# ScalarE instead of VectorE copies the transposed rows out of PSUM in the projections, and the query pieces go ahead of the keys' cast

## What is computed

```python
qh = split_heads(layernorm(x) @ Wq + bq)      # 16 x 512 x 256
kh = split_heads(ctx @ Wk + bk)               # 16 x 1601 x 256
vh = split_heads(ctx @ Wv + bv)
scores = einsum('bhqd,bhkd->bhqk', qh, kh) * 16 ** -0.5
out = einsum('bhqk,bhkd->bhqd', sparsemax(scores), vh)
x = x + tanh(g_xattn[0]) * (merge_heads(out) @ Wo + bo)
x = x + tanh(g_ffn[0]) * moe(layernorm(x))    # 8 experts, the best 2 of each row
```

## Time and profile before

| | us |
|---|---|
| median of 3 runs | 6868.18 |
| lowest and highest | 6863.97, 6875.29 |
| the profiled execution | 6908.67 |
| its span, first to last instruction | 6906.8 |

### The profile page before, as it was taken

One profiled execution on the slowest core, in us unless ns is written; L12 is line 12 of the kernel. 1 busy time (PEld: TensorE's weight loads), 2 busy tenths in 40 slices (PEclk: granted clock), 3 DMA queues, 4 the chain that ended last, 5 costly groups with the idle time before them and its releaser, 6 DMA issues. The chain is left out here.

```text
span 6906.8 us, 164803 instructions
## 1 busy us (share of the span) xinstructions
PE 5085.9 (74%) x19554; PEld 1673.0 (24%) x19555; DVE 6013.8 (87%) x50066; ACT 5556.3 (80%) x12484; POOL 2471.6 (36%) x10299
## 2 busy tenths in 40 slices
PE   8895777776777677676777777777777777767695
PEld 5551111111111111111111111111111111136574
DVE  4558999999999999999999999999999999957445
ACT  3336998998999999898999999999999999942221
POOL 2222333333333333333333333333333333324432
PEclk9995676676667766666766676666666676677798
DMA  5762111111111111111111111111111111145235
GB/s 194 238 201 56 30 34 29 31 35 28 31 31 32 31 31 31 30 30 29 28 31 32 31 32 31 33 29 31 31 35 32 32 32 33 28 152 207 89 100 204
DMA packets 691615, 415.98 MB, mean 60 GB/s; under 512 B 503712, under 2 KB 597536, under 8 KB 690208
## 3 DMA queue, kind: packets, MB, share of 16 engines
q1 hardware_dynamic: 677408, 370.58, 21.4%
q0 software_dynamic: 13056, 35.74, 1.4%
HBM read 249.13 MB, written 156.88 MB: 59 GB/s over the span
## 5 line engine op out<-in xcount | busy, mean ns | idle before, releaser
L887 DVE MAX8 a_cand<-a_scores 128x8 f32<-128x42 f32 (+1 forms) x38912 | 4395.9, 199 | 176.8 <-issue 140.9
L633 ACT ACTIVATE a_junk_act<-a_cand,a_ntau 128x304 f32<-128x304 f32 (+1 forms) x3840 | 1933.4, 522 | 145.2 <-POOL a_ntau L964 49.7
L603 PE MATMUL a_ring<-a_q,a_k 99*128 99x512 bf16 (+1 forms) x3328 | 1472.0, 556 | 764.1 <-ACT a_scores L669 499.3
L548 PE MATMUL a_out<-a_attn,a_v 128*32 128x512 f32 (+1 forms) x6656 | 1418.0, 793 | 518.8 <-ACT a_attn L673 518.8
L669 ACT COPY a_scores<-a_ring 128x1024 f32<-128x1024 f32 (+1 forms) x2048 | 1611.3, 830 | 154.0 <-PE a_ring L599 83.5
L673 ACT ACTIVATE a_attn<-a_ring 128x1024 f32<-128x1024 f32 (+1 forms) x1792 | 1654.1, 975 | 52.1 <-PE a_ring L603 50.9
L599 PE MATMUL a_ring<-a_k,a_q 96*128 96x512 bf16 (+1 forms) x4096 | 1336.5, 454 | 75.9 <-DVE a_ident L700 33.7
L633 ACT ACTIVATION_READ_ACCUMULATOR a_junk_act<-a_cand,a_ntau 128x1 f32 x3840 | 798.5, 208 | 0.0
L599 PEld LDWEIGHTS a_ring<-a_k,a_q 96*128 96x128 bf16 x4096 | 385.9, 116 | 1427.6 <-ACT a_attn L673 646.2
L603 PEld LDWEIGHTS a_ring<-a_q,a_k 99*128 99x128 bf16 (+1 forms) x3328 | 286.9, 118 | 1603.2 <-ACT a_scores L669 877.5
L548 PEld LDWEIGHTS a_out<-a_attn,a_v 128*32 128x32 f32 (+1 forms) x6656 | 174.4, 122 | 1189.0 <-ACT a_attn L673 718.9
(11 more groups left out here) (232 smaller groups left out, 6369.2 us busy)
## 6 DMA issues: line engine op xcount, KB each, us to landing
a_k<-k_parts SPq DMA_DIRECT2D x1536, 50.0 KB
k_parts<-p_ks SPq DMA_DIRECT2D x48, 800.5 KB, 7.3
o_parts<-a_o SPq DMA_DIRECT2D x512, 64.0 KB, 1.6
e_o<-o_parts SPq DMA_DIRECT2D x64, 512.0 KB
p_ctx<-in_ctx_t SPq DMA_DIRECT2D x16, 1601.0 KB, 8.6
v_heads<-p_v SPq DMA_DIRECT2D x16, 1536.0 KB
a_q<-q_parts SPq DMA_DIRECT2D x1536, 16.0 KB
a_v<-v_heads SPq DMA_DIRECT2D x256, 96.0 KB
```

The costliest lines, as they stand in the source:

```text
L548: mm = nc.tensor.matmul(out_ps[at:at + 2 * HEAD_DIM], beside, attn[0:rows, k, (c % 2) * BANK:(c % 2 + 1) * BANK], start=first and c < 4, s ...
L603: mm = nc.tensor.matmul(at[0:rows, m * BANK:(m + 1) * BANK], k_st[0:SCORE_ROWS + TAU_ROWS, ut, c * P:c * P + rows], q_st[0:SCORE_ROWS + TA ...
L633: ins = nc.scalar.activation(into[:, t].rearrange("p (a b) -> p a b", b=CHUNKS), cand[:, u % SLOTS, t, 0:w], ACT.Relu, bias=ntau[:, u % 2, ...
L887: ins = V.max(cand[:, u % SLOTS, t, :, c], scores[:, u % SLOTS, t, lo:hi])
```

## The change

Three things change, all in `project_program`:

1. ScalarE copies the two `turn` banks into `xnt`, at the head of its batch. VectorE no longer does. The counts of both semaphores follow: `job_used_dve` counts 13 jobs a batch in place of 15, `job_used` 12 in place of 10.
2. ScalarE takes the two `q` banks right after the `k` banks and the square root. The keys' cast, with its wait for the keys' store, comes behind them and just ahead of the queries' cast.
3. In `norm`, VectorE waits for TensorE's two transposes of the current batch before it writes `xn` anew (`turns_made`). The wait for `q_high` at the head of VectorE's batch is gone.

```diff
-        by_dve = [j[0] in ("turn", "v") for j in jobs]
+        by_dve = [j[0] == "v" for j in jobs]
...
                             if job[1] == 0:
-                                pe.wait_ge(job_used_dve, b * dve_jobs + HALVES)
+                                pe.wait_ge(job_used, b * act_jobs + HALVES)
...
             def batch(b, last=False):
                 for n, job in enumerate(jobs):
-                    if job[0] == "k":
+                    if job[0] == "turn":
+                        act.wait_ge(job_made, NJ * b + n + 1)
+                        nc.scalar.copy(xnt[:, job[1]], ring[:, n % RING]).then_inc(job_used, 1)
+                    elif job[0] == "k":
...
                             if not last:
                                 root(b + 1)
-
-                            act.wait_ge(job_used, readers_before(b, n + 1)[1])
-                            act.wait_ge(k_stored, 48 * b)
-                            nc.scalar.copy(ks[:, 0], kf[:]).then_inc(k_high, 1)
...
                         if a == HALVES - 1:
                             act.wait_ge(job_used, readers_before(b, n + 1)[1])
+                            act.wait_ge(k_stored, 48 * b)
+                            nc.scalar.copy(ks[:, 0], kf[:]).then_inc(k_high, 1)
                             act.wait_ge(q_stored, 48 * b)
                             nc.scalar.copy(qs[:, 0], qf[:]).then_inc(q_high, 1)
...
-            def norm(b, u, n_loaded):
+            def norm(b, u, n_loaded, turns_made):
...
-
+                if turns_made is not None:
+                    dve.wait_ge(job_made, turns_made)
                 for t in range(TILES):
                     nc.vector.tensor_scalar(xn[:, t], xt[:, u, t], moments[:, t, 0:1], rstd[:, t:t + 1], ALU.subtract, ALU.mult).then_inc(normed, 1)
...
             def batch(b, u, g, last=False):
-                for n, job in enumerate(jobs):
-                    if job[0] == "turn":
-                        if job[1] == 0:
-
-                            dve.wait_ge(q_high, b)
-                        dve.wait_ge(job_made, NJ * b + n + 1)
-                        nc.vector.tensor_copy(xnt[:, job[1]], ring[:, n % RING]).then_inc(job_used_dve, 1)
-
                 if not last:
-                    norm(b + 1, 1 - u, g + 1 + u)
+                    norm(b + 1, 1 - u, g + 1 + u, NJ * b + HALVES)
```

More of the change, by code:

```diff
@@ L346, in batch @@
                     nc.vector.tensor_tensor(s[:, 2], r[:], s[:, 1], ALU.subtract).then_inc(split, 1)
-            norm(0, 0, 1)
+            norm(0, 0, 1, None)
             with dve.Fori(0, BATCH // 2 - 1) as g:
```

## The result

The changed kernel takes **6948.89 us** (median of 4 runs, 6940.7 to 6951.73) against 6867.3 us before (4 runs, 6863.97 to 6875.29). The ratio is 1.0115, with a 95% interval of 1.0098 to 1.0133. The forecast was 6885 and the range ended at 6899: the direction was right, the size was not.

A forecast was written before the change was run, and what follows sets the result against it. The prediction took VectorE's ring through the values' store (30.88 us a lap) to bound the projections. Half clock +18.9, batch 0 +0.4 and last batch −1.9 gave +17.4 us: median 6868.2 to 6885 us, range 6862 to 6899.

The forecast's parts named there:

- the moved gap: TensorE's 2.21 us wait at the keys becomes a 3.6 us wait at the sixth value job.
- Which ring binds: Projections: VectorE's cycle through the values' store sets the 30.88 us lap; TensorE's is at most 0.2 us behind.
- The store's piece: Projections: from VectorE's key split to its next first value copy, which waits for the values' store, 15.64 us a lap.
- Where the gap goes: TensorE's wait leaves the keys for the sixth value job, growing from 2.21 to 3.6 us, ended by VectorE's value copy.
- The price of the gap: Value jobs: one half-clock stretch a lap costs 1.1 to 1.6 us, taken as 1.35; 14 laps give +18.9 us.
- slow twice: Rival: in the projections the clock stays at half for a second stretch, 14 x 3.2 − 1.5 = +43 us, 6911; chance 0.08.
- The last batch: End of projections: value copies take 8.1 us in place of 10.0 with TensorE ahead, −1.9 us.
- Batch 0: First projections batch: the keys' cast comes 3.4 us later and pushes `qr` past the split, +0.4 us once.
- ScalarE's copies and the new wait for `turns_made` at nothing: Projections: ScalarE's two copies (1.3 us) and VectorE's wait for the transposes add 0 us on the path.
- The attention runs the same instructions before and after: Attention stage: all that the change touches lies in the projections, so the attention stays unchanged.
- The signs of being wrong: Projections: first value copy under 15 us after the key split, gap at values under 2 us, or clock at 1.00 there.
- 40 us longer … nearly all outside the part that changes: Whole kernel: the profiled execution exceeds the median by 40 us, nearly all outside the projections; carried over as it is.

The follow-up runs named there:

- e1: The changed kernel with 12 empty instructions at the end of VectorE's part of the projections: 6902.12 us.
- e8: The changed kernel with 1 empty instruction at the end of VectorE's part of the projections: 6902.08 us.
- e7_before_vfirst: The kernel before with SyncE's two stores of the values moved ahead of those of queries and keys, nothing of the change: 6945.48 us.
- e6_turn_only: The changed kernel with the keys' cast moved back ahead of the query pieces, plus 12 empty instructions: 6885.85 us.
- e9_keys_first: The changed kernel with 12 empty instructions, values stored first, and keys ahead of queries in VectorE's splits and SyncE's stores: 6796.32 us.

## Why the prediction was wrong, point by point

Two steps failed. The forecast put the attention at no change, and it lost some 47 of the 82 us of the medians, by where its code lies. And it priced the moved gap at 1.35 us a lap, where 2.4 were measured. That the direction came out right is by the forecast's mechanism for 34 us only; the larger part had no term in the sum, so for it the direction was luck.

- **Which ring binds**: right. The store's piece is 238 us in 15 laps before and after, and opening it took the projections of the changed kernel from 568 to 476 us. No copy that left VectorE moved it.
- **Where the gap goes**: right. It left the keys and stands at the sixth value in all 15 laps, ended by VectorE's value copy, 62.1 us in total. Its size was 3.6 us in the sum and about 4 us in the rows (3.97 above). TensorE's way from the transposes to the values is 15.5 us (349.3 to 364.79) and not the 15.9 of the earlier trace rows: the laps of before at full clock have 18.1 us there, 2.6 more, of which the gap's row names only 2.2.
- **The price of the gap**: the step that failed in the projections. "I take 1.35 us, the middle" was the estimate for one slow stretch a lap. Batches 1 to 14 paid 33.9 us, 2.4 each: five paid 1.4 to 1.7, as I had said, and nine 2.5 to 3.1, because the clock was still at half for a second stretch. The rival "slow twice" had 3.2 us a lap and 0.08, with the remark that no stretch of more than 3.4 us was to be seen before. But before had no gap of 4 us in these laps either. The rows bounded a gap of 2.2 us, and I used them as the bound for one nearly twice as long. The point at which the clock falls was read from one lap too: 2.4 us after TensorE stopped there, 2.3 to 3.9 over the ten laps of before, and 2.9 to 5.3 in after. Even so this term alone, 6902 us as e1 and e8 show, would have missed the range by only 3 us.
- **The last batch**: −1.9 us forecast, −0.2 measured. It had its slow stretch too, and the store's piece grew by 0.8.
- **Batch 0**: +0.4 forecast, +1.2 measured. The query split waited 0.6 us for `qr` as worked out, and the first value copy was 0.6 us later, which I hadn't seen.
- **ScalarE's copies and the new wait for `turns_made` at nothing**: right; neither shows in a wait of the binding ring. The keys' cast was still released by the keys' store, 14 times, 27.8 us in all.
- **"The attention runs the same instructions before and after"**: true and beside the point. The step from the same instructions to the same time failed, and it was the larger part, 52.5 of 87 us by the stages. One program per engine holds all stages, and 12 instructions fewer in one shift the loop heads of the next. Nothing in my sum stood for that, and no rival did.
- **The signs of being wrong**: none of the three came. The first value copy was as late as before, the gap was over 2 us and the clock fell. They looked at the ring alone, and so could not tell that the price was off, or that another stage had moved. The lines that failed were "laps of 32 to 32.5 us" (32.4 to 36.0) and "the attention unchanged".
- **"40 us longer … nearly all outside the part that changes"**: right; it was the experts' stage, and it didn't come again.

## What to carry to other kernels

Ask of a gap that is to be removed where it will stand afterwards. A gap that another wait hides can cost nothing, and the same gap moved to the pace-setting stretch costs its clock. And when a change shortens or lengthens an engine's program ahead of a hot loop, compare the stages one by one: a stage whose code is the same can move by 1%, and a few instructions of padding tell whether that is placement. Where a ring through a store binds, try the order of the stores together with the change and without it: the same new order took 95 us off the changed kernel (with its 12 instructions) and cost the kernel before 78.

## What the runs showed of the hardware that I had not expected

- The branch back of the attention's loop costs VectorE a pause of some 2.9 us; that of its loops with 129 and 142 instructions a turn costs 0.3 us at most. With the head in an unlucky place a second pause of 2.4 to 3.2 us follows behind its first instruction: 19 times, 52 us, switched on by 116 instructions on one kernel and off by 1 or 12 on the other.
- How often half clock follows a gap of TensorE isn't told by the gap's length. After 2.2 us it followed in 10 of 15 laps of before, and after the same gap at the keys in 4 of 15 of `e7_before_vfirst`. It followed all 15 gaps of after (2.7 to 6.0 us), with 5.0 to 6.2 us of it in the value jobs in nine laps and 2.9 to 3.4 in six. In `e6_turn_only` four gaps of 3.0 to 3.5 us were free. With nine filler matmuls in the gap of after it came once, with no gap (`e9_keys_first`) never.
- One small-piece store of the values holds SyncE's queue for 6.2 to 8.5 us while it is issued, in before and after (5.2 in the last two batches), and what stands behind it in that queue starts that much later. Put early, it let the query stores start only 6.5 to 7.2 us after the query split in batches 0 to 13 of the kernel before, and 0.2 to 1.0 us after it in batches 1 to 13 of the changed one.
- The releaser named for a stall can be an artefact: at the branch back it was `a_attn` in one trace and `a_scores` in the other, at one and the same place.
